# First microseconds of an eight-core macaron layer: products of constants ahead of x, the first chunk's sums reordered, one centring of V2 moved

## The reference, cut to what matters

```python
def _L0_ffn_ref(x, U1, V1, b1, U2, V2, b2):       # D_MODEL 1024, D_FF 4096, RANK 256
    P = jnp.einsum('bsd,dr->bsr', x, U1)
    H = jax.nn.gelu(jnp.einsum('bsr,rf->bsf', P, V1) + b1)
    Q = jnp.einsum('bsf,fr->bsr', H, U2)
    return jnp.einsum('bsr,rd->bsd', Q, V2) + b2
...
    x = x + 0.5 * _L0_ffn_ref(_layernorm(x, axis=-1), ...)
    x = x + _L0_attn_ref(_layernorm(x, axis=-1), ...)
    x = x + 0.5 * _L0_ffn_ref(_layernorm(x, axis=-1), ...)
```

## Time and profile before

| | us |
|---|---|
| median of 3 runs | 876.81 (876.78 to 903.51) |
| the profiled execution | 876.68 |
| its span, slowest core (core 7) | 875.1 |
| spans of the eight cores | 871.3 to 875.1 |
| TensorE busy in that span | 821.2 |
| ScalarE, VectorE, GpSimd busy | 636.8, 466.4, 167.0 |

### The profile page before, as it was taken

How to read it: one execution, slowest core, us unless ns; L and a number is a source line. 1 busy time by engine, 2 the same in 40 slices (tenths; PEclk the granted TensorE clock), 3 DMA queues, 4 the chain that set the end, 5 groups by cost and what they waited for, 6 DMA issues and landing times.

```text
span 875.1 us, 13105 instructions; the slowest of 8 cores (871.3 to 875.1 us)
## 1 busy us (share of the span) xinstructions
PE 821.2 (94%) x4122; PEld 397.4 (45%) x4122; DVE 466.4 (53%) x735; ACT 636.8 (73%) x803; POOL 167.0 (19%) x192
## 2 busy tenths in 40 slices
PE   4899999999899999999999999999989969999997
PEld 1344444444445455464554545544434424444442
DVE  2466665656565744746447474374553470445352
ACT  2667675768566898999999898989646526766764
POOL 0220400003231212313123131221231220031100
PEclk9899999999999999999999999999999999999999
DMA  8899301000041002200012000227000010122122
GB/s 266 265 324 322 54 2 49 1 2 1 1 119 40 1 1 55 78 25 1 1 61 73 25 1 1 75 73 239 26 1 1 1 41 8 46 64 88 22 97 96
DMA packets 17929, 57.83 MB, mean 66 GB/s; under 512 B 2116, under 2 KB 3524, under 8 KB 17352
## 3 DMA queue, kind: packets, MB, share of 16 engines
q1 hardware_dynamic: 17864, 57.00, 21.6%
HBM read 43.35 MB, written 13.64 MB: 65 GB/s over the span
## 4 chain that ended last, share of the span: by engine, by line
PE 85%; DVE 6%; ACT 4%; issue 3%; DMA 1%; DVEq 0%; SPq 0%; POOL 0%; ACTq 0%; POOLq 0%
PE ps L1036 13%; PE ps L271 13%; PE ps L1074 12%; PE ps L673 12%; PE ps L254 6%; PE ps L256 6%; PE ps L822 6%; PE ps L1235 6%; PE ps L195 4%; PE ps L227 2%; ACT pt L1049 2%; PE ps L730 1%; PE ps L289 1%; PE ps L291 1%; DMA x<-x 1%
## 5 line engine op out<-in xcount | busy, mean ns | idle before, releaser
L1049 ACT ACTIVATE pt<-ps,small 128x1024 bf16<-128x1024 f32 x320 | 321.8, 1026 | 97.6 <-PE ps L1036 91.3
L261 ACT ACTIVATE hb<-ps,cols 128x512 bf16<-128x512 f32 x256 | 171.3, 686 | 80.2 <-PE ps L256 79.3
L1036 PE MATMUL ps<-QZ,KM 128*128 128x512 bf16 (+1 forms) x640 | 177.1, 358 | 2.0 <-ACT pt L1049 1.8
L1074 PE MATMUL ps<-pt,V 128*128 128x512 bf16 (+3 forms) x640 | 170.3, 348 | 0.9 <-POOL V L884 0.9
L1058 POOL TENSOR_TENSOR pt<-pt,cb 128x256 bf16<-128x256 bf16 x128 | 87.3, 694 | 335.6 <-ACT pt L1049 335.6
L673 PE MATMUL ps<-yb,wqk 128*128 128x512 bf16 x512 | 140.3, 382 | 4.2 <-DVE small L734 1.5
L1074 PEld LDWEIGHTS ps<-pt,V 128*128 128x128 bf16 x640 | 62.5, 98 | 66.6 <-issue 2.1
L1036 PEld LDWEIGHTS ps<-QZ,KM 128*128 128x128 bf16 x640 | 61.1, 98 | 61.8 <-issue 13.7
L271 PE MATMUL ps<-hb,u2b 128*128 128x512 bf16 x256 | 76.5, 384 | 3.7 <-ACT hb L261 2.1
L271 PE MATMUL ps<-hb,u2c 128*128 128x512 bf16 x256 | 75.3, 379 | 1.8 <-ACT hb L261 1.4
L822 PE MATMUL ps<-wvb,yb 128*128 128x256 bf16 x512 | 73.5, 272 | 1.9 <-DVE small L734 1.2
(11 more groups left out here) (134 smaller groups left out, 876.5 us busy)
## 6 DMA issues: line engine op xcount, KB each, us to landing
x<-x SPq DMA_DIRECT2D x16, 512.0 KB, 13.2
out<-x SPq DMA_DIRECT2D x32, 256.0 KB, 2.4
stg<-u SPq DMA_DIRECT2D x10, 512.0 KB, 10.9
stg<-v SPq DMA_DIRECT2D x10, 512.0 KB, 10.8
wos<-wo SPq DMA_DIRECT2D x8, 512.0 KB, 4.2
wst<-wq SPq DMA_DIRECT2D x7, 512.0 KB, 4.0
wst<-wk SPq DMA_DIRECT2D x7, 512.0 KB, 4.3
wst<-wv SPq DMA_DIRECT2D x6, 512.0 KB, 10.2
```

The costliest lines, as they stand in the source:

```text
L261: F["t_gelu"][g] = ACT.do(lambda e: e.activation(F["hb"][:, g % 4, :], ps[:, b, :], AF.Gelu_apprx_tanh, bias=cols[:, C_B1 + fc:C_B1 + fc + ...
L1036: f = lambda e, j=j, kt=kt: e.matmul(ps[:, 2 * sl + j, lo:TC], KM[s][:, 128 * kt:128 * (kt + 1)], QZ[s][:, h, TC * c + lo:TC * (c + 1)], s ...
L1049: t_e[i] = ACT.do(lambda e: e.activation(pt[:, i % 4, :, lo:TC], ps[:, 2 * sl:2 * sl + 2, lo:TC], AF.Exp, bias=bias, scale=0.125))
L1074: f = lambda e, kt=kt, lo=lo, j=j: e.matmul(ps[:, b, lo:TC], V[gr % 2][:, kt, pr, 64 * h:64 * h + 128], pt[:, i % 4, j, lo:TC], start=(kt ...
```

## The change

Four edits, all ahead of or inside the first chunk.

1. `warm(n)` issues n products of two constants (`ones` and the 128x512 constant tile) into bank 4, which nobody reads: 6 ahead of U1's column means, 3 in their middle, 8 behind them, 3 behind the first sum, 10 behind the last U1 product of the first chunk.
2. On VectorE the centring of U1's second half moves from ahead of quarter 1's cast to ahead of quarter 3's. On TensorE the products of the first chunk are put in a written-out order, in which the sums stand ahead of the products with U1 where the data allow it and the last two pairs of squares ahead of the last U1 products. The products of quarters 0 and 1 with U1 wait for the first half of U1 alone. The last square is VectorE's instead of ScalarE's.
3. Of chunk 1's quarters only the first is loaded ahead of the stream; the other three move to steps 1, 5 and 9, one `load_v1u2` later than before each. Their casts move from steps 18, 20, 23, 26 to 19, 21, 24, 26.
4. `center_v2` of the second half moves from step 31 of chunk 0 to step 2 of chunk 1.

```diff
-    def center_v2():
+    F1["t_v2"], F1["t_v2r"] = [], []
+
+    def center_v2(*rs):
-        F1["t_v2"], F1["t_v2r"] = [], []
-        for r in range(2):
+        for r in rs:
...
     PE.need(t_cb)
+
+    def warm(n):
+        for _ in range(n):
+            PE.run(lambda e: e.matmul(ps[:, 4, :], ones, cbf[:, :, :], start=True, stop=True))
+
+    warm(6)
     for k in range(NM):
+        if k == 4:
+            warm(3)
         PE.need(u1_cast[k // 4])
...
     cast0 = [ln_cast(0, 0, xb0, t_x[0][0])]
-    DVE.need(t_cs)
...
-    cast0 += [ln_cast(0, i, xb0, t_x[0][i]) for i in range(1, 4)]
-    sq0 = [ln_square(ACT, i, xb0, cast0[i], None, sq) for i in range(4)]
+    u1_center(0)
+    cast0 += [ln_cast(0, i, xb0, t_x[0][i]) for i in range(1, 3)]
+    u1_center(1)
+    cast0.append(ln_cast(0, 3, xb0, t_x[0][3]))
+    sq0 = [ln_square(ACT if i < 3 else DVE, i, xb0, cast0[i], None, sq) for i in range(4)]
...
-    for i in range(4):
-        t1 = pair_mm(5, lambda k: ones, xb0, i, cast0[i])
-        if i == 3:
-            t2 = pair_mm(6, lambda k: ones, sq, i, sq0[i])
+    def first_mean(i):
+        return pair_mm(5, lambda k: ones, xb0, i, cast0[i])
+
+    def first_square(i):
+        return pair_mm(6, lambda k: ones, sq, i, sq0[i])
+
+    def first_p(i):
         for m in range(2):
-            tk[m] = pair_mm((7, 3)[m], lambda k, m=m: u1b[:, k, 128 * m:128 * (m + 1)], xb0, i, F1["t_u1"])
-        if i < 3:
-            pair_mm(6, lambda k: ones, sq, i, sq0[i])
+            tk[m] = pair_mm((7, 3)[m], lambda k, m=m: u1b[:, k, 128 * m:128 * (m + 1)], xb0, i, F1["t_u1"][i // 2])
+
+    warm(8)
+    first_mean(0)
+    warm(3)
+    first_square(0)
+    first_p(0)
+    first_mean(1)
+    first_p(1)
+    first_square(1)
+    first_mean(2)
+    t1 = first_mean(3)
+    first_p(2)
+    first_square(2)
+    t2 = first_square(3)
+    first_p(3)
+    warm(10)
     sq_free = t2
...
-    for i in range(2):
-        load_x(1, i)
+    load_x(1, 0)
...
     put(0, 1, load_v1u2, 4)
-    put(0, 1, load_x, 1, 2)
+    put(0, 1, load_x, 1, 1)
     put(0, 5, load_v1u2, 5)
-    put(0, 5, load_x, 1, 3)
+    put(0, 5, load_x, 1, 2)
     put(0, 9, load_v1u2, 6)
+    put(0, 9, load_x, 1, 3)
...
-    for i, s in enumerate((18, 20, 23, 26)):
+    for i, s in enumerate((19, 21, 24, 26)):
         put(0, s, ln1_prep, 1, i)
...
-    put(0, 31, center_v2)
+    put(0, 31, center_v2, 0)
+    put(1, 2, center_v2, 1)
```

More of the change, by code:

```diff
@@ L409, in build_nc, with u1_center @@
     cast0 = [ln_cast(0, 0, xb0, t_x[0][0])]
-    DVE.need(t_cs)
     F1["t_u1"] = []
-    for i in range(2):
-        t = DVE.do(lambda e, i=i: e.tensor_tensor(
+    def u1_center(i):
+        DVE.need(t_cs)
+        t = DVE.do(lambda e: e.tensor_tensor(
             u1b[:, 4 * i:4 * i + 4, :], stg[:, u1_st[i][0], :].rearrange("p (c r) -> p c r", c=4),
@@ L417, in build_nc @@
         st_free[u1_st[i][0]] = t
-    bank_free[0] = t
-    cast0 += [ln_cast(0, i, xb0, t_x[0][i]) for i in range(1, 4)]
-    sq0 = [ln_square(ACT, i, xb0, cast0[i], None, sq) for i in range(4)]
+        bank_free[0] = t
+    u1_center(0)
[3 more added lines that the diff above has]
+    sq0 = [ln_square(ACT if i < 3 else DVE, i, xb0, cast0[i], None, sq) for i in range(4)]
     def pair_mm(b, lhs, tiles, i, ready):
@@ L434, in build_nc @@
     tk = [None, None]
-    for i in range(4):
-        t1 = pair_mm(5, lambda k: ones, xb0, i, cast0[i])
-        if i == 3:
-            t2 = pair_mm(6, lambda k: ones, sq, i, sq0[i])
-        for m in range(2):
-            tk[m] = pair_mm((7, 3)[m], lambda k, m=m: u1b[:, k, 128 * m:128 * (m + 1)], xb0, i, F1["t_u1"])
-        if i < 3:
-            pair_mm(6, lambda k: ones, sq, i, sq0[i])
+    def first_mean(i):
[3 more added lines that the diff above has]
+    def first_p(i):
+        for m in range(2):
+            tk[m] = pair_mm((7, 3)[m], lambda k, m=m: u1b[:, k, 128 * m:128 * (m + 1)], xb0, i, F1["t_u1"][i // 2])
[14 more added lines that the diff above has]
+    warm(10)
     sq_free = t2
-    t_r = ln_rstd(0, 1, ln_var(0, 5, t1, 6, t2, None))
     t_mu = {}
@@ L454, in build_nc @@
     L = {"sqf": sq_free, ("c", 0): cast0}
+    t_r = ln_rstd(0, 1, ln_var(0, 5, t1, 6, t2, None))
     keep_mean(0, 5, t1)
```

## The result

| | before | after |
|---|---|---|
| median, us | 878.07 (876.42 to 957.03, 6 runs) | 872.27 (871.9 to 874.85, 6 runs) |
| ratio | | 0.9949 (95%: 0.9928 to 0.9971) |
| profiled execution: spans of the eight cores | 871.3 to 875.1 | 867.1 to 869.8 |
| their mean | 873.3 | 868.4 |

The new kernel is 0.5% faster, 2.5 to 6.3 us by the interval. Of the page of after, whose slowest core is core 1, two lines. The first is the busy time, the second the shares of the chain that ended last; in it the DMA has 4%, where it had 1% before (on another core, the slowest there): the loads have become a limit.

The account below looks back on a forecast made before the run. Bounds: a chain until 27.12 us, then TensorE with the loads right behind, then TensorE save Q's eviction. 2.6 us at step 28 plus 1.4 at V2 make 4.0: 876.8 to 872.8 us; 8-in-10 range 870.3 to 875.8.

Parts of the forecast that it names:

- the sum: Whole kernel: 2.6 us at step 28 plus 1.4 us at V2 make 4.0 us, 876.8 to 872.8; chance 0.57.
- its largest term: Step 28 on core 7 moves from 53.24 to 50.6: 2.6 us of the 5.2 that the head won.
- The clock and the head: First chunk: clock rises at about 12 us, variance starts at 19.7 not 23.36, first V1 product at 23.4 not 27.12.
- The gap in the queue: DMA between 22 and 26 us: part 3's load issued at 21.6 instead of 25.32, closing 2.0 us of idle time.
- One place in the queue, 1.8 us: V1's parts 4, 5 and 6 load one place earlier, 1.8 us each; part 7 stays 13th.
- the wait at step 24: TensorE waits for V1's part 6, landing at 44.9: step 24 at 45.7 instead of 43.3.
- V2's second half, 1.4 us: Start of chunk 1: Q's eviction no longer waits behind that centring on VectorE; 1.4 us net.
- The shift should reach the end: Behind 72 us: order fixed and TensorE busy, so the 4.0 us should arrive whole at the kernel's end.
- Only Q's eviction: Rival: the head's gain is lost whole to late loads; only 1.4 us remain, 875.4; chance 0.17.
- The loads keep up: Rival: V1's parts come before TensorE wants them, the head's whole gain passes, 6.6 us, 870.2; chance 0.13.
- Nothing: Rival: warm products don't raise the clock early; with a late V2, 876.3 to 877; chance 0.06.
- The granted clock: Rival: busier cores bring more products at a lowered clock, 0.045 us each; 879, up to 886; chance 0.05.

Follow-up runs that it names:

- e2: The changed kernel with its 30 warm products not issued; 872.19 us, ratio 0.9968 to the kernel before.
- e1: The kernel before with edit 4 alone (centring of V2's second half moved to chunk 1); 873.93 us against 875.24, ratio 0.9985.
- e10: The kernel before with 27 warm products alone (6, 3, 8 and 10); 876.65 us against 875.70, ratio 1.0008.
- e12: e10 without the first six warm products and with seven instead of ten at the end (18); 874.27 us, ratio 0.9991 to the kernel before.
- e3: The changed kernel with edit 3 undone, x's quarters of chunk 1 loaded and cast in the old order; 872.66 us, ratio 0.9974 to the kernel before.
- e4: The changed kernel with V1's part 7 loaded ahead of x's quarter 3 of chunk 1; 870.48 us, ratio 0.9956 to the kernel before.
- e7: The changed kernel once more, unchanged, on another chip; 873.16 us against 875.70 for the kernel before, ratio 0.9965.
- e5: The changed kernel without loading part 7 of V1 and U2, whose casts reread part 6 (wrong weights); 876.15 us, ratio 1.0003 to the kernel before.
- e6: The changed kernel with edit 2 undone (first chunk in the old order, 27 warm products); 873.26 us, ratio 0.9977 to the kernel before.
- e11: e10 with three more warm products behind the first sum (30); 875.70 us against 876.03 for the kernel before, ratio 1.0002.
- e8: e4 with the cast of part 7 two steps sooner and two subtractions moved behind quarter 3's square; 871.83 us, ratio 0.9952 to the kernel before.
- e9: e8 with GpSimd's two copies of V2 waiting for chunk 1's last square; 871.07 us, ratio 0.9947 to the kernel before.

## Why the prediction was right

The time, 872.3, is 0.5 us under the 872.8 of the sum. The difference was 4.5 us by the ratio (2.5 to 6.3) against 4.0, and 3.1 on the other chip. The mechanism held: the head gains, the loads take part of it back at step 28, and Q's eviction adds its own. How near the number came is in part luck: the base of its largest term was 0.7 us too high, as the last point but one says. By its steps:

**The clock and the head: right.** On core 7 the rise came among the eight products behind the column means, as placed; on the eight cores it came from 6.8 to 12.5 us, on three of them before 7.4, and on core 3 the clock fell once more, from 10.2 to 13.6, and V1 came last (24.49). The variance started at 19.90 against 19.7, the first V1 product at 23.67 against 23.4, with 0.85 us idle against one, and at the high level. The last square on VectorE took 0.69 and came before its turn.

**Which edit earns it: the sum took them together, and the runs show an overlap.** At V1's first product the warm products alone bring 2.0 us; the new order without them 1.9 us (e2); both together 2.8 to 3.0. At step 28, against e1, the warm products alone bring 0.9 to 1.2 (e10 to e12), the order and the loads without them 1.3 (e2), all together 1.8 to 2.0: the parts add up to more than the whole.

**The gap in the queue: right.** Part 3's load was issued at 21.86 against 21.6, and the DMA's share between 22 and 26 rose to 0.92. What closing it is worth is read from e3 against e1, which have the same order of loads: parts 4 to 7 land 1.8, 2.7, 2.1 and 1.9 us sooner on the mean, against the 2.0 of the sum.

**One place in the queue, 1.8 us: right in size, and still the wait at step 24 did not come.** Parts 4, 5 and 6 land 1.6, 1.0 and 2.2 us sooner in after than in e3, which has them a place later; part 7 in e4, 2.9 us sooner than in after. From 26 us on in after, all cores together, a part of the weights lands 1.7 us behind the load before it on the mean, a quarter of x 2.0 us, each from 1.2 to 3.4, so that one place on one core can be far from the price. The price that the prediction worked out from the Trainium skill ("DMA: Bandwidth & Descriptors", Where 436 GB/s comes from), 1.46 us as an estimate, is under both means: core 7 moved 282 to 356 GB/s in slices of 4 us, less than the 358 of the page. Part 6 landed at 42.8 on core 7, not 44.9, and on the mean 4.3 us sooner than in e1, not 3.8. So TensorE's waits near 45 came on two of eight cores only (0.4 and 0.8 us), and six waited for a cast of V1 once, at step 28. That cost the sum nothing, because part 7 kept its 13th place: it landed at 49.98 on core 7, 2.0 us sooner than before, and the step that the sum rested on is step 28: 50.91 against 50.6.

**Edit 3: not priced on its own in the prediction beyond the place that it moves.** It takes away the wait for part 6 that e3 shows on all cores (1.0 to 2.7 us), and the wait for part 7 stands right behind it: by itself it measures nothing in e3. e4 moves part 7 too and gets 1.6 us. This is the point at which the argument could have gone further: it named the load that ends last and did not ask which edit touches it.

**V2's second half, 1.4 us: right**, 1.40 in the marks of after and of e1 alike, 1.2 in e1's mean span.

**"The shift should reach the end": not quite.** The prediction costed the 30 products at nothing, with the idle time of TensorE as their cover. Part of their cost is 860 us later: on core 4 of after the block landed at 863, among the stores, and it was 6.6 us from the last product to the end (core 5 took 6.0 without one). On all other cores it came behind the end or not at all, and the mean of that stretch was 5.2 us in after and 4.7 in e7, against 4.6. What this step left out is that the added instructions are also code that has to be loaded. In this kernel the stretch is 0.1 to 0.7 us longer for it at most, in e10 1.4.

**The base.** The execution from which all steps start had its die 1 at a granted clock of 0.84 from 40 to 49; the prediction itself put it at 1.3 us on core 7, and left it in the base. It did not name the two later dips (0.82 from 54 to 59 and from 86 to 91). On the four cores without them, before to after, step 28 moved by 2.0 us (52.92 to 50.93), and against e1 by 1.8 to 2.0. By the mean spans of all runs of e7 and e1 the whole change is worth 3.1 us, of which edit 4 has 1.2: 1.9 for the head, not 2.6. The 2.6 was right for the marks that it was read from and some 0.7 too large for the kernel's usual run. That it came true on the eight cores (2.64) is luck of the base.

**The rivals.** Only Q's eviction: excluded by step 28, 1.8 us or more sooner than in e1, and by e7's mean span, 3.1 us against the 1.2 of edit 4 alone. The loads keep up: excluded, TensorE waits for part 7 on every core, from 0.3 to 3.35 us. Nothing: excluded by the interval. The granted clock: it was 0.89 to 0.97 on the four cores of die 0 in after, from 30 to 40 and from 40 to 49, and 1.00 from 49 to 56. Those cores then waited 0.3 to 1.7 us for part 7, and so the slower products had mostly used time that would have been waited away. It ended by itself, as before.

## What to carry to other kernels

When a head gets faster and loads stand behind it, find the one load that is waited for last and move that one: moving part 7 by one place (e4) gave 1.6 us, nearly as much as edits 1 to 3 together (1.9). Look for the second one behind it, which may be as late within half a microsecond (e3). Read a gain from a base whose clock was steady, or from a second execution: a dip of one die's clock made 2.6 us out of 1.9. And look at where the code of added instructions is loaded: 54 instructions that nobody waits for brought a load among the last stores, and in e10 1.4 us of the gain went there.

## What the runs showed of the chip

**A wait can cost the clock as well, on some cores.** After step 28's wait, core 6 of after:

```profile
50.26 0.59 PE L254 MATMUL ps<-pb,v1b 128*128 128x512 bf16 x1 [2.39 <-DVE v1b L348]
50.63 0.63 PE L256 MATMUL ps<-pb,v1b 128*128 128x512 bf16 x1
51.06 3.10 PE L195 MATMUL ps<-yb,cb 128*128 128x512 bf16 x8
53.99 1.89 PE L195 MATMUL ps<-sq,cb 128*128 128x512 bf16 x8
```

The eight sums took 2.93 us, where core 7 took 1.72 after a longer wait (3.35 us). The granted clock of core 6 was 0.76 between 49 and 56, that of core 7 1.00. It happened on one of eight cores in after, on four in e7, five in e5, two in e10 and one each in e3, e6, e11 and e12; on none in e4, e8 and e9, whose longest wait is 1.6 us. The shortest wait that went with such a fall was 1.97 us (e5), the longest that didn't the 3.35 us above. The length of the wait alone doesn't decide it, and what does stays open.

**GpSimd's casts double VectorE's.** An instruction of VectorE between SBUF tiles (cast, square or subtraction) that starts under one takes 1.33 to 1.55 us instead of 0.69: all 25 of them in after between 26 and 58 us, all cores together, and none that starts elsewhere (VectorE of core 7 of after, with GpSimd's cast of a part of U2 running from 44.71 to 45.91):

```profile
44.93 1.52 DVE L518 TENSOR_TENSOR x<-x,mu 128x512 f32<-128x512 f32 x1
46.37 0.68 DVE L179 CAST yb<-x 128x1024 bf16<-128x1024 f32 x1
```

**Code is loaded through the DMA engines too,** and in e10 the stores next to one such load of 0.02 MB stood still for about 1 us, far longer than its size explains at the 350 to 400 GB/s around it. Why they do, and what sets the moment at which the block is loaded, stays open.
